# Delta rule: the 32-blocks' inverses are merged by 32x32 products, a projection stands between the merge's two steps, and memory sets have their own waiters

## What is computed

```python
q = l2norm(silu(conv(x @ Wq)));  k = l2norm(silu(conv(x @ Wk)));  v = silu(conv(x @ Wv))
def step(S, inp):                        # per head, token by token
    qt, kt, vt, gt, bt = inp
    S = S * jnp.exp(gt)
    delta = (vt - kt @ S) * bt
    S = S + kt[:, None] * delta[None, :]
    return (S, qt @ S)
```

## Time and profile before

| | us |
|---|---|
| median of 3 runs (lowest, highest) | 2015.58 (2011.38, 2016.25) |
| the profiled execution | 2014.03 |
| its span, first to last instruction | 2012.1 |
| TensorE busy over the span | 1594.2 (79%) |
| VectorE, GpSimd, ScalarE busy | 1044.1, 686.5, 657.8 |

### The profile page before, as it was taken

The page is one execution under the profiler, slowest core; times in us unless marked ns, Lnnn a source line. Parts: engine busy times, 40 slices in busy tenths (PEclk is TensorE's granted clock), DMA queues, the critical chain, the costliest instruction groups (busy, mean ns, idle before and its releaser), DMA issues. The chain is left out here.

```text
span 2012.1 us, 28647 instructions
## 1 busy us (share of the span) xinstructions
PE 1594.2 (79%) x10592; PEld 1052.7 (52%) x10666; DVE 1044.1 (52%) x2374; ACT 657.8 (33%) x1166; POOL 686.5 (34%) x1093
## 2 busy tenths in 40 slices
PE   4787786878699968587999999999999674777771
PEld 3354444544356644235656666666666563455651
DVE  3756455463224436554676666766667222335523
ACT  3061431623222215442445444454444111111010
POOL 3020200200000000157786767777676701000152
PEclk8999898998889979798999999999999666887696
DMA  1000000000020032302312233121321103120273
GB/s 52 1 2 1 21 2 11 12 1 12 12 86 22 11 96 96 63 16 38 53 23 45 40 53 54 27 48 33 54 48 34 29 7 109 47 68 32 51 166 101
DMA packets 216894, 84.21 MB, mean 42 GB/s; under 512 B 166265, under 2 KB 211682, under 8 KB 216770
## 3 DMA queue, kind: packets, MB, share of 16 engines
q1 hardware_dynamic: 205330, 68.10, 15.1%
q0 software_dynamic: 5376, 12.59, 2.4%
q10 hardware_dynamic: 6064, 1.86, 0.4%
HBM read 50.80 MB, written 31.72 MB: 41 GB/s over the span
## 5 line engine op out<-in xcount | busy, mean ns | idle before, releaser
L1810 DVE SCALAR_TENSOR_TENSOR d_conv<-d_prep,k_cw,d_conv 128x511 f32<-128x511 f32 (+2 forms) x288 | 214.3, 746 | 32.7 <-ACT d_conv L1641 26.0
L1762 POOL TENSOR_TENSOR d_prod<-d_blk 64x30 f32<-64x30 f32 (+4 forms) x360 | 172.9, 480 | 105.0 <-DMA d_blk<-mid_a_blk 77.8
L1427 PE MATMUL d_prep<-k_hT,k_w 128*128 128x512 f32 x384 | 191.1, 623 | 21.5 <-POOL d_power L1736 12.4
L1766 POOL TENSOR_TENSOR d_blk<-d_blk,d_prod 64x30 f32<-64x30 f32 (+4 forms) x360 | 183.7, 510 | 28.2
L424 ACT ACTIVATE a_probs<-a_acc 128x896 f32<-128x896 f32 x128 | 117.1, 918 | 172.5 <-PE a_acc L248 107.6
L523 DVE TENSOR_REDUCE a_top<-a_turn 128x4 f32<-128x512 f32 (+3 forms) x240 | 147.1, 652 | 47.9 <-PE a_turn L210 40.5
L471 POOL TENSOR_TENSOR a_rstd<-a_rstd,a_mhalf 128x4 f32<-128x4 f32 x4 | 4.1, 1027 | 368.6 <-DVE a_rstd L575 368.6
L1427 PEld LDWEIGHTS d_prep<-k_hT,k_w 128*128 128x128 f32 x384 | 68.6, 198 | 83.0 <-issue 49.1
L1641 ACT ACTIVATE d_conv<-d_prep,k_cw 128x512 f32<-128x512 f32 x96 | 65.9, 686 | 133.9 <-PE d_prep L1427 133.5
L1466 PE MATMUL d_prep<-d_kq 128*128 128x256 f32 x384 | 95.0, 392 | 16.0 <-DVE d_qkT L1842 15.3
L1466 PEld LDWEIGHTS d_prep<-d_kq 128*128 128x128 f32 x384 | 73.0, 197 | 44.8 <-DVE d_qkT L1842 27.1
(11 more groups left out here) (353 smaller groups left out, 3592.2 us busy)
## 6 DMA issues: line engine op xcount, KB each, us to landing
mid_gate<-p_gate SPq DMA_DIRECT2D x4, 768.0 KB, 3.4
mid_v<-p_v_tok SPq DMA_DIRECT2D x4, 768.0 KB, 3.5
d_v_h<-mid_v SPq DMA_DIRECT2D x12, 256.0 KB, 5.6
d_gate_h<-mid_gate SPq DMA_DIRECT2D x12, 256.0 KB, 5.4
mid_a_blk<-d_AT SPq DMA_DIRECT2D x48, 64.0 KB, 2.0
d_blk<-mid_a_blk SPq DMA_DIRECT2D x12, 256.0 KB, 3.7
mid_u_blk<-d_blk SPq DMA_DIRECT2D x12, 256.0 KB, 2.9
mid_l_blk<-d_blkT SPq DMA_DIRECT2D x12, 256.0 KB, 3.7
```

Of the source, the lines that this page charges most:

```text
L1427: last = nc.tensor.matmul(PB[f % 2][:], w[:, n % 2, i, k, :], hT[:, k, b * T:(b + 1) * T], start=k == 0, stop=k == CK - 1)
L1762: nc.gpsimd.tensor_tensor(pr, blk[:, 0:t, t:t + 1].broadcast_to([lanes, t, m]), blk[:, t:t + 1, t + 1:BLK].broadcast_to([lanes, t, m]), AL ...
L1766: nc.gpsimd.tensor_tensor(blk[:, 0:t, t + 1:BLK], blk[:, 0:t, t + 1:BLK], pr, ALU.subtract).then_inc(subst, 1)
L1810: ins = nc.vector.scalar_tensor_tensor(dst, PB[f % 2][:, 0:T - j], cw[:, n % 2, f % 2, TAPS - 1 - j:TAPS - j], dst, ALU.mult, ALU.add)
```

## The change

Level 2 computes only the quarters that are used, by 32x32 products in the strips of the array that belong to their rows and columns, and both L's and U's quarter directly, so that `level2_u` with its transposes goes. `U32` and `L32` go too: the inverted blocks are gathered straight into `U` and `L`. ScalarE and VectorE take two batches each of L's and U's quarters, four copies of 32x128 a batch. `project(q + 1, 0)`, the first projection of the head after next, moves from the first step of `recur` to between level 2's steps, with ScalarE's scale and VectorE's convolution. The gather now waits for the last solve of the head before and for its X3 products. The wait for six memory sets becomes three semaphores, waited for where they are used: `ones_set` (TensorE's first sum), `powers_set` (GpSimd), `cleared` (`U`, `L`, `X2`; set by GpSimd behind its second spread). The last two spreads of head 1 move from GpSimd to VectorE (`spread_first`, into the same buffers). The diff, without the declarations:

```diff
@@ -1349,6 +1350,7 @@
         ORDER = (0, 3, 1, 2)
+        PAIRS = [(slice(64 * k, 64 * k + BLK), slice(64 * k + BLK, 64 * k + 2 * BLK)) for k in range(2)]
         block = ctx.enter_context(nc.Block())
@@ -1381,12 +1383,15 @@
                 sp.wait_ge(inv_out, 32 * n + 32)
+                if n == 0:
+                    sp.wait_ge(cleared, 3)
                 if n:
-                    sp.wait_ge(l2_e, BATCH * n)
+                    sp.wait_ge(x3, BATCH * n)
+                    sp.wait_ge(solved, CH * n)
                 for j in range(NB):
                     r = slice(BLK * j, BLK * (j + 1))
-                    sp.dma_start(U32[r, :, r], u_blk[j, :, :, :].rearrange("c s t -> s c t")).then_inc(inv_back, 16)
-                    sp.dma_start(L32[r, :, r], l_blk[j, :, :, :].rearrange("c s t -> s c t")).then_inc(inv_back, 16)
+                    sp.dma_start(U[r, :, r], u_blk[j, :, :, :].rearrange("c s t -> s c t")).then_inc(inv_back, 16)
+                    sp.dma_start(L[r, :, r], l_blk[j, :, :, :].rearrange("c s t -> s c t")).then_inc(inv_back, 16)
@@ -1413,8 +1418,6 @@
         def _(pe):
-            pe.wait_ge(consts, 6)
-
             def project(n, f):
@@ -1422,14 +1425,17 @@
                 elif n:
-                    pe.wait_ge(attn, 8 * n)
+                    pe.wait_ge(attn, 8 * n - 1 + f)
                 for k in range(CK):
...
             def sum_squares(n, b):
-                if b == 0 and n:
-                    pe.wait_ge(n_half, 2 * n)
+                if b == 0:
+                    if n:
+                        pe.wait_ge(n_half, 2 * n)
+                    else:
+                        pe.wait_ge(ones_set, 1)
                 if b == 2:
@@ -1446,7 +1452,10 @@
             def differences(n, b):
-                pe.wait_ge(gu_ready, BATCH * n + b + 1)
+                if n == 1 and b >= 2:
+                    pe.wait_ge(gu_first, b - 1)
+                else:
+                    pe.wait_ge(gu_ready, BATCH * n + b + (1 if n < 1 or n == 1 and b < 2 else -1))
                 if b or n:
@@ -1467,11 +1476,6 @@
-            def times(b, left, right):
-                for c in range(CH):
-                    last = nc.tensor.matmul(LB[b][:, c, :], left[:, b * CH + c, :], right[:, b * CH + c, :], start=True, stop=True)
-                return last
-
             def turn_out(n, c):
@@ -1492,22 +1496,24 @@
                 pe.wait_ge(k_ready, BATCH * n + i + 1)
-                times(ORDER[i], AT[:, n % 2, :, :], L32).then_inc(x2, 1)
+                b = ORDER[i]
+                for c in range(CH):
+                    for r, q in PAIRS:
+                        last = nc.tensor.matmul(LB[b][q, c, r], AT[r, n % 2, b * CH + c, q], L[r, b * CH + c, r], start=True, stop=True)
+                last.then_inc(x2, 1)
...
                 pe.wait_ge(x2_e, BATCH * n + i + 1)
-                times(ORDER[i], U32, X2).then_inc(l2, 1)
-
-            def level2_u(n):
-                for i, b in enumerate(ORDER):
-                    pe.wait_ge(l2_e, BATCH * n + i + 1)
-                    for c in range(CH):
-                        last = nc.tensor.transpose(LB[b][:, c, :], L[:, b * CH + c, :], ident[:])
-                    last.then_inc(u2, 1)
+                b = ORDER[i]
+                for c in range(CH):
+                    for r, q in PAIRS:
+                        nc.tensor.matmul(LB[b][q, c, r], U[q, b * CH + c, q], X2[q, b * CH + c, r], start=True, stop=True)
+                        last = nc.tensor.matmul(LB[b][r, c, q], X2[q, b * CH + c, r], U[q, b * CH + c, q], start=True, stop=True)
+                last.then_inc(l2, 1)
...
                 for i, b in enumerate(ORDER):
-                    pe.wait_ge(u2_e, BATCH * n + i + 1)
+                    pe.wait_ge(lu_act if i % 2 == 0 else lu_dve, BATCH // 2 * n + i // 2 + 1)
                     pe.sem_inc(carrier)
@@ -1543,9 +1549,10 @@
                         level2_x(m, i)
+                    if q + 1 < D_H:
+                        project(q + 1, 0)
                     for i in range(BATCH):
                         level2_l(m, i)
-                    level2_u(m)
                     level3(m)
@@ -1572,7 +1579,7 @@
                         turn_out(n, c - 1)
-                    if ahead:
+                    if ahead and c:
                         project(n + 2, 2 * c)
@@ -1607,8 +1614,6 @@
         def _(act):
-            act.wait_ge(consts, 6)
-
             def silu(n, f):
@@ -1663,14 +1668,13 @@
                 ahead = n + 2 < D_H
-                if ahead:
-                    begin(n + 2)
                 for c in range(CH):
...
                     if ahead:
-                        convolve(n + 2, 2 * c)
+                        if c:
+                            convolve(n + 2, 2 * c)
                         convolve(n + 2, 2 * c + 1)
@@ -1697,6 +1701,8 @@
                 b = ORDER[i]
+                if n == 0 and i == 0:
+                    act.wait_ge(cleared, 3)
                 act.wait_ge(x2, BATCH * n + i + 1)
@@ -1707,12 +1713,20 @@
                         decay_up(q, b)
+                ahead = q + 1
                 if 0 <= m < D_H:
...
                         keep_x2(m, i)
-                    for i, b in enumerate(ORDER):
-                        act.wait_ge(u2, BATCH * m + i + 1)
-                        nc.scalar.activation(U[:, rows[b], :], LB[b][:], ACT.Copy).then_inc(u2_e, 1)
+                    for i in (0, 2):
+                        b = ORDER[i]
+                        act.wait_ge(l2, BATCH * m + i + 1)
+                        for r, q in PAIRS:
+                            cut(L[:, rows[b], :], LB[b], q, r)
+                        for r, q in PAIRS:
+                            cut(U[:, rows[b], :], LB[b], r, q, lu_act if r.start else None)
+                    if ahead < D_H:
+                        begin(ahead)
+                        convolve(ahead, 0)
                     for i, b in enumerate(ORDER):
@@ -1730,11 +1744,14 @@
         def _(pool):
-            for m, value in ((U32, 0.0), (L32, 0.0), (X2, 0.0), (ones, 1.0), (mhalf, -0.5)):
-                nc.gpsimd.memset(m[:], value).then_inc(consts, 1)
+            nc.gpsimd.memset(ones[:], 1.0).then_inc(ones_set, 1)
             nc.gpsimd.memset(power[:, 0, :], 0.5)
-            nc.gpsimd.memset(power[:, 1, :], -0.5).then_inc(consts, 1)
-            pool.wait_ge(consts, 6)
+            nc.gpsimd.memset(power[:, 1, :], -0.5)
+            nc.gpsimd.memset(mhalf[:], -0.5).then_inc(powers_set, 1)
+
+            def clear_blocks():
+                for m in (U, L, X2):
+                    nc.gpsimd.memset(m[:], 0.0).then_inc(cleared, 1)
@@ -1774,14 +1791,14 @@
             spread(0, 1)
+            clear_blocks()
             spread(0, 2)
             spread(0, 3)
+            pool.wait_ge(powers_set, 1)
             raise_norms(0)
...
             substitute(0)
-            spread(1, 2)
-            spread(1, 3)
             raise_norms(1)
@@ -1799,7 +1816,6 @@
         def _(dve):
-            dve.wait_ge(consts, 6)
             vec = lambda t: t[:, :, None].broadcast_to([P, TILES, D_V])
@@ -1858,7 +1874,11 @@
                 dve.wait_ge(l2, BATCH * n + i + 1)
-                nc.vector.tensor_tensor(L[:, rows[b], :], LB[b][:], L32[:, rows[b], :], ALU.add).then_inc(l2_e, 1)
+                for r, q in PAIRS:
+                    nc.vector.tensor_copy(L[q, rows[b], r], LB[b][q, :, r])
+                for r, q in PAIRS:
+                    ins = nc.vector.tensor_copy(U[r, rows[b], q], LB[b][r, :, q])
+                ins.then_inc(lu_dve, 1)
@@ -1908,6 +1928,11 @@
+            def spread_first(b):
+                dve.wait_ge(diff, BATCH + b - 1)
+                nc.vector.tensor_tensor(g_upto[:, b % 2, :, :], upto[:, None, :].broadcast_to([P, CH, P]),
+                                        g[:, 1, b * CH:(b + 1) * CH, None].broadcast_to([P, CH, P]), ALU.mult).then_inc(gu_first, 1)
+
             def gate_out(n):
@@ -1936,6 +1961,8 @@
                         weigh(q, f)
+                        if q == 1 and f % 2:
+                            spread_first(2 + f // 2)
                 if invert:
@@ -1951,8 +1978,10 @@
                 if invert:
-                    for i in range(BATCH):
-                        keep_l(m, i)
+                    keep_l(m, 1)
+                    keep_l(m, 3)
+                    if q + 1 < D_H:
+                        convolve(q + 1, 0)
```

More of the change, by code:

```diff
@@ L1311, in layer1_delta_rule @@
         prod = sb("prod", [NB * TILES, BLK * BLK // 4])
-        U32, L32 = sb("U32", [P, TILES, P]), sb("L32", [P, TILES, P])
         U, L = sb("U", [P, TILES, P]), sb("L", [P, TILES, P])
@@ L1328, in layer1_delta_rule @@
         LB = [pb(f"rec{n}", [P, CH, P]) for n in range(4)]
-        (consts, proj, scaled, conved, silued, squared, summed, nsum_ready, n_turned, n_half, n_ready, pow_ready,
+        (ones_set, powers_set, cleared, proj, scaled, conved, silued, squared, summed, nsum_ready, n_turned, n_half, n_ready, pow_ready,
```

(8 more changed lines are left out.)

## The result

The changed kernel takes 1998.34 us in the median (1996.05 to 2003.24, 4 runs) against 2013.53 for the kernel before in the same runs: a ratio of 0.992, 95% interval 0.990 to 0.994. That is 15 us faster, where 45 were forecast. The profiled execution took 2003.24 us, 10.8 less than that of before. Of this the delta rule gives 16.7 less; code that did not change, ahead of it and behind it, took 5.9 more in this execution.

What follows compares the result with a forecast made beforehand. TensorE was taken as the bound, 62.18 us a head. Nine heads 37.5, start 5.5 and head 11 2, together 45 us off 2014.03, gave 1969, as a median 1970; range 1950 to 1997.

Steps and rivals of the forecast that it cites:

- Level 2: Small passes at 16 ns, evictions setting the end: first solve at 9.7 instead of 15.04 us, 5.3 less a head.
- Rivals 2, 4 and 5: Products one after the other, 1995 (0.18); small pass costs like 64x64, 2046 (0.06); no change, only the start gained (0.04).
- The start: With the memory sets' own waiters, TensorE's first projection starts with GpSimd's first memset: 5.5 us gained.
- Head 1's spreads: Last two spreads moved to VectorE: TensorE's 10.54 us wait only moves to the inverted blocks' DMA, worth 0.
- The new waits: SP's gather waiting for the fourth solve of the recurrence before costs nothing: the solve starts over 5 us early.
- The clock: From L/U to the first solve, one stretch at 1.2 GHz a head: 1.55 us lost, bounds 0 and 4.
- Rival 3: Clock stays at 1.2 GHz through levels 2 and 3, 4 us a head instead of 1.55: 1996; chance 0.08.
- GpSimd's loop: The loop beside TensorE takes 56.7 us against 61.8, 5.1 to spare, so TensorE at 58.0 remains the bound.
- Rival 1: GpSimd's loop becomes the bound at 56.7 us, each level 2 released by the DMA filling L: 1957; chance 0.22.
- Heads 10 to 11 and 11: Period before head 11 hangs on GpSimd's loop in both kernels, 0; head 11 gains 2 us (bounds 5 and 0).

Runs made afterwards that it cites:

- e_fill4: Changed kernel with four added full-width TensorE products of 128 columns a head, results unread, nothing left out: 1984.9 us, ratio 0.981 to 0.988.
- e_half_subst: Changed kernel with every second step of GpSimd's substitution left out, so the 32-blocks are not inverted: 1941.6 us, ratio 0.963 to 0.969.
- cand_act: Changed kernel with the sign folded into the substitution (GpSimd's negation gone) and the transposed copy moved from GpSimd to ScalarE: 1988.2 us.
- e_half_collide: Changed kernel with every second substitution step left out, plus two spare GpSimd operations a head beside `gate_out`: 1976.4 us.

## Why the prediction was wrong

*Level 2*: right. 16 ns a pass was taken, X measured 17.7; 9.7 us to the first solve, 9.58 measured in undisturbed heads, ended by ScalarE as said. Rivals 2, 4 and 5, which need 32 ns a pass and more, fall: two products in different strips overlap in the same PSUM bank. The rule of the Trainium skill ("TensorEngine Tiling (Array Packing)", Restrictions and Gotchas), by which they would not, isn't borne out here; at 32 ns X would have taken 2.05, not 1.13.

*The start*: 5.5 at its place, as forecast, but with head 0 to 1 longer by 2.1 (the bound that I gave head 0), so 3.4 remain.

*Head 1's spreads*: right, 0; the stall went to the DMA ahead of head 0's level 2 (17.25 us, about 10 forecast).

*The new waits*: right. In heads 1 to 10 SP waits only for GpSimd, VectorE and its own DMAs, and not for a solve.

*The clock*: a term mis-sized, and by place the larger part of what is missing. One short stretch a head, 1.55 us, bounds 0 and 4, was read from one row. Heads 1, 5 and 8 took 7.3 us each over 56.5, with 17 us at 1.2 GHz, beyond the upper bound. The nine heads took 37.6 over 9 x 56.5: these three 21.9; in the other six the longer products of `gate_out` make 6.7, and the 9.0 that are left go with shorter stretches at 1.2 GHz. So the clock took some 31 us where 14 were put, and the collision 6.7 where nothing was. By e_fill4 keeping the stretches short is worth 13 us in all. Rival 3 (the clock stays down in levels 2 and 3, 4 us a head, 1996) has the right time, nearly the right mean (31 over nine heads are 3.4) and nearly the right place: it falls in level 3 and stays down in the recurrence, but in three heads only. That the time agrees is in part luck. It had 0.08.

*GpSimd's loop*: the step that failed, and by the experiments what set off both losses in heads 1 to 10. I wrote that the loop had 5.1 us to spare against TensorE's 61.8, and compared lengths only: 58.0 against 56.7, so TensorE remains the bound. That the loop's closing operations would then run beside `gate_out`, 2 us on VectorE's way to the next head, was not looked for, though both places are in the trace of before (1.9 to 5.2 us apart). With the loop shortened (e_half_subst) the nine heads took 522.4 us, and the forecast's 9 x 58.0 is 522: what was missing in heads 1 to 10 comes back when the loop is short, the long stretches at 1.2 GHz included. Rival 1 named the engine (0.22) and priced it as a bound of 56.7, with each level 2 released by the DMA as its sign; only those of heads 0 and 11 are. The loop acts sooner, by the collision and by moving the place where the clock falls.

*Heads 10 to 11 and 11*: head 11 gave 2.45 against 2. The period before it hangs on the loop, as said, but took 2.8 more: from SP's spread to GpSimd's first product 9.9 us, 7.4 before. The profile's DMA queues, from 1.5 us behind the spread's start, after and before:

```profile
q1 hardware_dynamic: 1461, 0.18, 21.7%
q8 instruction: 1, 0.02, 2.5%
...
q1 hardware_dynamic: 3221, 0.66, 68.5%
```

In the changed kernel a load of instructions (one packet of 16 KB, 2.21 us) runs beside the spread's last store there, and that store's last 66 packets start 1.5 us behind the others; before, none runs. Over all the traces SP went on 3.5 to 3.8 us behind the spread's start wherever no such load ran beside it, and up to 6.5 where one did; e_half_subst has one here too (2.04 us, and 9.7 to the first product). That fits, but no run moved the load, so the cause is not shown.

What could not be separated: in the changed kernel the collision and the clock's loss go together, so 13 for the clock and 24 for the loop in heads 1 to 10 overlap. The collision isn't needed for a long stretch: head 0 of e_half_subst and cand_act have them without it. Why the clock falls 8 us behind level 2's start in one head and 16 in the next isn't settled either; heads of equal length repeat their place.

## What to carry to other kernels

When the engine at the bound becomes faster, don't only compare its new period with the next loop's: lay that loop's last operations against the new timeline and see what they then run beside. Small products that save TensorE's time can lose it again through the clock, so leave full-width work between them, and count its passes before adding any. A loop just below the bound should be shortened with the change, not after it.

## What the runs showed of the hardware

Two products of VectorE with both inputs in SBUF, 0.69 us each, took up to 2.19 beside a GpSimd operation that reads SBUF, and GpSimd's 2.00 became 2.49. Whichever began later waited: in the changed kernel VectorE's first product began 0.37 us behind GpSimd's and ended 0.36 behind its end; in e_half_collide VectorE's began first and kept its 0.69. The Trainium skill, "SBUF — State Buffer", "Who interferes with whom", says that a VectorE instruction with two SBUF inputs contends with a GpSimd instruction that reads SBUF. The trace agrees; the later one did not wait for the other's end and then take its whole 0.69 us, but ended 0.36 to 0.38 behind it.

The transposed copy of 64x1024 took ScalarE 1.99 us and GpSimd 2.00; a straight 128x1024 activation takes ScalarE 1.06. 128 passes of 32x32 in four strips were issued within 1.9 us, waits included; 117 of them, with no wait between, within 1.05, 9 ns each.
